# Second layer's attention: maxima's tiles padded with zeros to 128 partitions and columns, and the maxima rounded and split with two small reductions

## The reference, cut to what matters

```python
qk, v = jnp.split(x @ W_emb.T, 2, axis=-1)          # 16 heads of 64
anchor_B = qk @ W_anchor.T * SCALE                   # b, head, n, 64 anchors
attn = jax.nn.softmax(anchor_B, axis=-1)             # over the anchors
s = jnp.sum(attn, axis=-2)
out = jnp.einsum('bhna,bhnd->bhad', attn, v)         # gathered per anchor
out = recip[..., None] * out                         # recip = 1 / s
out = jnp.einsum('bhna,bhad->bhnd', attn, out)
return out.transpose(0, 2, 1, 3).reshape(b, n, INNER) @ W_out.T + b_out
```

## Time and profile before

| | |
|---|---|
| Median of 3 runs | 780.24 us (776.69 to 781.25) |
| Profiled execution, first to last instruction | 778.5 us |
| Mean granted TensorE clock, as a share of 2.4 GHz | 0.926 |
| TensorE matmuls busy | 654.1 us, 84% |
| VectorE busy | 570.3 us, 73% |
| ScalarE busy | 400.4 us, 51% |
| GpSimd busy | 277.6 us, 36% |
| Attention loops, from the span's start | about 303 to 363, 434 to 477, 548 to 591, 662 to 705 us |

### The profile page before, as it was taken

The page is one execution under the profiler, slowest core; times in us unless marked ns, Lnnn a source line. Parts: engine busy times, 40 slices in busy tenths (PEclk is TensorE's granted clock), DMA queues, the critical chain, the costliest instruction groups (busy, mean ns, idle before and its releaser), DMA issues.

```text
span 778.5 us, 9648 instructions
## 1 busy us (share of the span) xinstructions
PE 654.1 (84%) x2985; PEld 470.0 (60%) x2985; DVE 570.3 (73%) x1441; ACT 400.4 (51%) x698; POOL 277.6 (36%) x229
## 2 busy tenths in 40 slices
PE   5777550399999995879989899899899899899897
PEld 2666540388878883446468555478555478556575
DVE  4889959279866736996976786866796866783763
ACT  3646233277777732334375444485443585442573
POOL 6457778200000026686202375211485120341100
PEclk9979755699999985989999999999999999999999
DMA  6441587778898610001000000000100000000000
GB/s 212 136 177 52 202 296 275 233 250 267 250 304 307 215 58 27 18 21 28 0 1 0 35 28 21 1 0 1 41 23 20 0 1 1 27 1 1 0 1 28
DMA packets 25779, 69.26 MB, mean 89 GB/s; under 512 B 5296, under 2 KB 8384, under 8 KB 24384
## 3 DMA queue, kind: packets, MB, share of 16 engines
q1 hardware_dynamic: 21632, 60.24, 23.0%
q0 software_dynamic: 4096, 8.40, 3.6%
HBM read 46.46 MB, written 22.16 MB: 88 GB/s over the span
## 4 chain that ended last, share of the span: by engine, by line
PE 58%; DVE 21%; POOL 7%; issue 6%; DMA 4%; ACT 4%; SPq 1%; DVEq 0%; ACTq 0%; POOLq 0%
PE ps L1685 14%; PE ps L1687 8%; PE ps L1681 8%; PE ps L1942 6%; PE ps L1689 6%; PE ps L1688 6%; DVE stats L1061 3%; POOL rows_by_expert L605 3%; PE ps L1960 2%; PE ps L1930 2%; DMA wbuf<-w_split 2%; DVE ring L1565 2%; DMA raw<-in_w 1%; DVE yb L1465 1%; DVE cmat L1641 1%
## 5 line engine op out<-in xcount | busy, mean ns | idle before, releaser
L652 POOL DMA_INDIRECT yb<-y_by_expert,ypos x64 | 63.3, 989 | 158.2 <-DMA y_by_expert<-ysb 142.6
L1685 PE MATMUL ps<-hid,fh 128*128 128x512 f32 x256 | 103.5, 404 | 5.1 <-DVE hid L1549 5.1
L1687 PE MATMUL ps<-hid,fh 128*128 128x512 f32 x256 | 101.4, 396 | 0.0
L605 POOL DMA_INDIRECT rows_by_expert<-h,pos x64 | 71.1, 1112 | 25.0 <-issue 18.9
L700 POOL TENSOR_TENSOR misc<-misc,ring 128x1024 f32<-128x1024 f32 x28 | 66.0, 2357 | 33.8 <-DVE ring L1539 28.7
L1549 DVE TENSOR_TENSOR hid<-ring,hid 128x512 fp32r<-128x512 f32 x56 | 38.6, 689 | 41.7 <-ACT hid L941 40.1
L1942 PE MATMUL ps<-ring,hn 128*128 128x512 f32 x112 | 56.5, 628 | 5.3 <-DVE ring L1539 5.3
L1685 PEld LDWEIGHTS ps<-hid,fh 128*128 128x128 f32 x256 | 48.2, 188 | 21.0 <-DVE hid L1549 10.3
L1960 PE MATMUL ps<-attnT,cmat 128*128 128x512 f32 x128 | 56.9, 592 | 0.0
L1687 PEld LDWEIGHTS ps<-hid,fh 128*128 128x128 f32 x256 | 48.3, 188 | 10.7
L998 ACT ACTIVATE ring<-ps 128x1024 f32<-128x1024 f32 x32 | 32.8, 1025 | 42.6 <-PE ps L1930 42.4
(11 more groups left out here) (326 smaller groups left out, 1702.4 us busy)
## 6 DMA issues: line engine op xcount, KB each, us to landing
wbuf<-w_split SPq DMA_DIRECT2D x46, 512.0 KB, 5.6
w_split<-parts SPq DMA_DIRECT2D x4, 2048.0 KB, 7.7
raw<-in_w SPq DMA_DIRECT2D x8, 512.0 KB, 8.5
xs<-rows_by_expert SPq DMA_DIRECT2D x16, 256.0 KB, 5.4
y_by_expert<-ysb SPq DMA_DIRECT2D x16, 256.0 KB, 4.5
ffn_raw<-in_ffn SPq DMA_DIRECT2D x1, 2816.0 KB, 11.1
rows_by_expert<-zeros SPq DMA_DIRECT2D x9, 256.0 KB, 2.5
xa<-in_x SPq DMA_DIRECT2D x4, 512.0 KB, 4.9
```

The costliest lines, as they stand in the source:

```text
L605: gp.indirect_dma_start(disp, bass.IndirectOffsetOnAxis(pos[:, b, k, t:t + 1].bitcast(U32), 0), h1[:, b % 2, t, :], None).then_inc(scatter ...
L652: gp.indirect_dma_start(yb[:, k, t, :], None, ydisp, bass.IndirectOffsetOnAxis(ypos[:, b, k, t:t + 1].bitcast(U32), 0))\
L1685: te.matmul(out_, w(0), x(0), start=first, stop=False)
L1687: return te.matmul(out_, w(0), x(1), start=False, stop=last_)
```

## The change

Three things are changed together.

- `m32`, `mTs` and `onehot` become 128 wide or 128 high. `m32` is filled with zeros once (a memset of 128x256 on VectorE behind the cast of `onehot`), and `oh_f` is made on 128 partitions. So the transpose of the maxima loads 128 columns of weights in place of 32, the copy moves 128 partitions, and the two matmuls of `shift` use 128 rows of weights in place of 32.
- `neg_max` writes the negated maxima straight into `m32[:, i, 32:48]`. The cast becomes a reduction with a maximum over one element, negated, which writes the rounded maximum (positive now) as fp32r. The subtraction becomes a reduction with a sum over the pairs (rounded, negated maximum). The first 16 rows of `onehot` become -1 to match. The negated maxima in columns 32 to 47 meet rows of `onehot` that are zero. The wait for the transpose of tile t-2 moves from ahead of the cast to ahead of the first reduction.
- `upto` moves into the arena, to make room.

```diff
-        onehot = sb("onehot", [32, 1024], F32R)
+        onehot = sb("onehot", [128, 1024], F32R)
-        mTs = sb("mTs", [32, 128], F32R)
+        mTs = sb("mTs", [128, 128], F32R)
-        nmax = sb("nmax", [128, 2, H])
-        m32 = sb("m32", [128, 2, 2 * H], F32R)
+        m32 = sb("m32", [128, 2, 128], F32R)
-        oh_f = at("oh_f", 48, [32, 1024])
+        oh_f = at("oh_f", 48, [128, 1024])
+        upto = at("upto", 78, [128, 2 * E, 2 * E])
...
-                gp.affine_select(out=v, in_=v, compare_op=ALU.not_equal, fill=1.0, base=base,
+                gp.affine_select(out=v, in_=v, compare_op=ALU.not_equal, fill=1.0 if base else -1.0, base=base,
...
-                copy(mTs[:, :], ps[0:32, 1, 0:128]).then_inc(*act_maxT.raise_(t))
+                copy(mTs[:, :], ps[:, 1, 0:128]).then_inc(*act_maxT.raise_(t))
...
             v.tensor_copy(onehot[:, :], oh_f[:, :])
+            v.memset(f(m32[:, :, :]), 0.0)
...
                 if t >= 2:
                     dve.wait_ge(*dve_max.now(t - 2, b))
-                settle(b, v.tensor_reduce(nmax[:, i, :], ps[:, k0:k0 + 2, :].rearrange("p k (h a) -> p (k h) a", a=A),
-                                          X, ALU.max, negate=True))
-                if t >= 2:
                     dve.wait_ge(*pe_maxT.now(t - 2, b))
-                settle(b, v.tensor_copy(m32[:, i, 0:H], nmax[:, i, :]))
-                v.tensor_tensor(m32[:, i, H:2 * H], nmax[:, i, :], f(m32[:, i, 0:H]), ALU.subtract)\
-                    .then_inc(*dve_max.raise_(t))
+                rounded, minus = m32[:, i, 0:H], f(m32[:, i, 2 * H:3 * H])
+                settle(b, v.tensor_reduce(minus, ps[:, k0:k0 + 2, :].rearrange("p k (h a) -> p (k h) a", a=A), X, ALU.max,
+                                          negate=True))
+                settle(b, v.tensor_reduce(rounded, minus.unsqueeze(2), X, ALU.max, negate=True))
+                both_ = f(m32[:, i, 0:4 * H]).rearrange("p (k h) -> p h k", k=2)[:, 0:H, :]
+                v.tensor_reduce(f(m32[:, i, H:2 * H]), both_, X, ALU.add).then_inc(*dve_max.raise_(t))
...
-                transposes(1, [f(m32[:, t % 2, :])], 32).then_inc(*pe_maxT.raise_(t))
+                transposes(1, [f(m32[:, t % 2, :])]).then_inc(*pe_maxT.raise_(t))
```

More of the change, by code:

```diff
@@ L160, in build @@
         thr = sb("thr", [128, E])
-        upto = sb("upto", [128, 2 * E, 2 * E])
         unit = sb("unit", [128, NT])
@@ L1677, in _, with transposes @@
             te = nc.tensor
-            def transposes(bank, srcs, rows_=128):
+            def transposes(bank, srcs):
                 for i, s in enumerate(srcs):
-                    last_ = te.transpose(ps[0:rows_, bank, i * 128:(i + 1) * 128], s, ident[:, :])
+                    last_ = te.transpose(ps[:, bank, i * 128:(i + 1) * 128], s, ident[:, :])
                 return last_
```

## The result

The changed kernel takes 770.68 us in the median of four runs (770.13 to 770.90), the kernel before 778.47 in the four runs that stand against it (776.00 to 781.25). The ratio is 0.9905, interval 0.9878 to 0.9931: 7.8 us less in the medians, 5.4 to 9.5 by the interval, just short of the 1% that a measurement of this kernel tells from no change. The profiled execution spans 768.4 us at a clock of 0.926, against 778.5 before.

What follows compares the result with a forecast made beforehand. TensorE was taken to bound mid-loop, VectorE and GpSimd the loop ends and first batch. Gains of 1.5 + 1.5 + 2.3 + 0.8 less 0.3 made 5.8 us, from 780.24 to 774.4; range 770.5 to 779.5.

Steps and rivals of the forecast that it cites:

- the rival without a collision: Attention loops: the gather L652 does not wait for VectorE's L1539; batches 2 and 3 gain 2.3 each, 772.1 us; chance 0.22.
- half of 0.22 and a fifth of 0.50: Shares of the no-collision rival's and the forecast's chances taken as below 772.4 us, over 1% faster; stated total 0.24.
- Part 1, rows: TensorE's `shift` matmuls: 128-row weights remove the idle gaps of 0.36, 0.38 us per tile, step from 5.15 to 4.77.
- The rival by which the gaps stay: TensorE's shift: the 0.36 gaps are not caused by 32 rows and remain; only the casts count, 778.8 us; chance 0.18.
- 4 x 0.38 = 1.5 us a batch: Attention loops: the shorter TensorE step counts for `shift(2)` to `shift(5)`, the four ahead of the last logits.
- Part 2: VectorE's maxima: reductions of 0.17 and 0.19 us never wait for GpSimd; 0.1 gained at tile 6, 0.7 at the last.
- What is late next, batches 2 and 3: Loop ends: L652 waits for L1539, so L700 starts 0.85 late; of 2.3 us, 1.5 is gained in each batch.
- First batch: First attention loop: the 2.77 us cast goes but GpSimd bounds next; 0.8 us gained.
- that of tile 7 follows directly: First loop's end: tile 7's L700 starts right behind tile 6's, which ends at 359.7, and runs until 362.05.
- The lock-step: GpSimd and VectorE catch each other every round: L1539 ends 1.1 behind L700, L652 0.83 behind that, as in first batch.
- the rival by which it also sets in in batches 2 and 3: Later loops: rounds take 5.55 instead of 5.15, 2.5 us lost in each of batches 2 and 3; 783.2 us; chance 0.10.
- Setup: Ahead of the loops: VectorE's memset precedes the L1414s and delays scatter L605; its whole time, 0.3 us, is added.

Runs made afterwards that it cites:

- after_again: The changed kernel, unchanged, run again on a second chip; ratio to the kernel before 0.9932, loops 55.08, 41.07, 41.07, 40.26 us.
- after_cols32: The changed kernel with the maxima's transposition writing 32 columns again and the copy 32 rows, the shift keeping 128 rows; ratio to the kernel before 0.9962.
- pad_only: The kernel before with the zeros and 128 rows and columns, the cast and the subtraction kept; ratio to the kernel before 1.0009.
- subtraction_kept: The changed kernel with the pair-sum reduction replaced by a tensor_tensor addition of 16 elements, the rounding still a reduction; ratio to the kernel before 0.9957.
- one_each: The changed kernel with one gather instead of two in rounds 3, 4 and 5, three left behind the last L700; ratio to the kernel before 0.9879.
- memset_only: The kernel before with only the 128x256 memset added ahead of the L1414s and `m32` widened to hold it; ratio to the kernel before 1.0030.
- reductions_only: The kernel before with the two reductions in place of cast and subtraction, 32 rows and columns, no memset; ratio to the kernel before 0.9983.

## Why the prediction was right, and where it was not

The time, 770.68, lies inside the range, 0.2 above its lower end and 3.7 under the forecast, outside the 772.5 to 776.5 that the forecast gave itself; by the number alone the rival without a collision (772.1) was nearer, and only the traces speak against it. The prediction's base was the median of three runs then shown, 780.24; with the runs of this comparison it is 778.47, which is 1.8 of the 3.7. Against 778.47 the gain was 7.8, not 5.8; after_again on another chip has 0.9932 of 802, 5.5. From the start of the first loop to the end the two traces differ by 469.93 - 464.20 = 5.7. The 0.3 that the forecast took off for the memset lies ahead of the loops, so its 6.1 for the loops stands against this 5.7. They are that near in part by luck: the loops gave 5.2, for the first fell short by 1.3, and 0.5 came between and behind the loops, where no term stood. What the whole time gained beyond 5.7, 2.1 in the medians and 4.4 in the traces, came ahead of the loops, where the prediction had a loss; its cause stays open. (A slip in the chances: half of 0.22 and a fifth of 0.50 make 0.21, not 0.24.)

- *Part 1, rows.* Right: both gaps gone, the step 4.79, 2.7 us less of matmuls for 7 tiles, 0.38 each, and the columns free (after_cols32). The rival by which the gaps stay is refuted.
- *Part 1, what it is worth.* "4 x 0.38 = 1.5 us a batch" as a term of its own was wrong. Alone it is worth 0.1 (pad_only). The step read the earlier trace rows and thought that TensorE, alone on the path in mid-loop, was the only bound; VectorE and GpSimd had a ring of 5.35 beside its 5.15, not on the path only because they had started with slack. The chain of waits doesn't show a second bound that near; the casts growing by 0.2 a tile did, had I asked why they grow.
- *Part 2.* 170 and 186 ns against 0.17 and 0.19; the last tile's wait gone. But the wait was put down to the cast. The subtraction would have taken it over (subtraction_kept), so the second reduction, costed at nothing gained, is worth 0.7 in batches 2 and 3 and 1.4 in the fourth.
- *What is late next, batches 2 and 3.* Right. `scaled(6)` was to end 2.3 earlier and did by 2.4 (34.02 behind the loop's start, against 36.42), the second gather ends 0.83 behind L1539 (the first one caught takes 1.76, the later ones 0.98, where 1.03 to 1.1 were given), L700 starts behind it, 1.6 is left instead of 2.4. Batch 4, without gathers, keeps 2.4 (forecast 2.3). one_each, which takes the collision away, brings the two to 40.28 too. This refutes the rival without a collision, and with it the Trainium skill's inference (SBUF — State Buffer, Who interferes with whom) that a tensor_tensor leaves the writing of descriptors alone: here the second L651 waits 0.8 for the end of a tensor_tensor.
- *First batch.* Wrong: 0.8 less was forecast, 0.5 more came (0.47 and 0.51 in two pairs of traces). The failed step is "that of tile 7 follows directly". The L700s come at the times worked out there, 5.57 apart against 5.55; but the last L1539 is itself caught:

```profile
352.56 3.94 DVE L1539 TENSOR_TENSOR ring<-ring,lrec 128x1024 f32<-128x1024 f32 x1
```
```profile
352.08 0.95 POOL L651 DMA_INDIRECT yb<-y_by_expert,ypos  x1 [0.30 <-issue]
353.05 2.35 POOL L699 TENSOR_TENSOR misc<-misc,ring 128x1024 f32<-128x1024 f32 x1
356.57 2.35 POOL L699 TENSOR_TENSOR misc<-misc,ring 128x1024 f32<-128x1024 f32 x1 [1.17 <-DVE ring L1539]
```

  It was issued 0.49 ahead of L699, but under the gather that runs until 353.03, and ends 1.1 behind L699; so the L699 of tile 7 starts 1.17 later than "directly". Measured from the loop's start, the L699 of tile 6 ends at 51.20, where the prediction has 51.1, and that of tile 7 at 54.72 against 53.45: these 1.17 are all but 0.1 of the miss. The prediction used these very 1.1 for every earlier tile. The lock-step that it saw in this loop thus ran on for one tile more; the rival by which it also sets in in batches 2 and 3 (0.10) did not come.
- *Setup.* The memset takes 0.27 (0.3 was taken). The scatter's end, 138.58, was read as just behind the last L1414's, but it stands 0.84 behind the third's. That its time is added whole was wrong: in the traces of the same two chips with it the scatter of 5.83 us is gone, 2.5 less up to the last scatter. How much of that reaches the end stays open; memset_only, with a ratio of 1.0030 [0.9990, 1.0070] on the first chip, excludes a gain of over 0.1% there, but its scatters had ended early.
- *Between the loops* the kernel after is 0.1 shorter each time, 0.4 in all; no term stood for it, and no run looked for its cause. It shows in every kernel that has the pads and the cast replaced, as far as no late gather stretches the time there (but for one stretch of 71.5 in after_cols32), and in neither pad_only nor reductions_only.

## What to carry to other kernels

A cheap operation that waits for another engine can hold a whole ring of waits together: ask of every stretched instruction whether its length grows from tile to tile, for then a second bound is just beside the first and edits to either alone give little. Where two edits remove two bounds that near, try the pair before throwing either away; here 0.1 and 0.5 a loop alone made 1.6 to 2.4 together. And when a wait goes, look at what it kept apart: the gathers that stood well before had to be moved to keep the whole gain.

## What the runs showed of the hardware that I had not expected

- A tensor_tensor of 16 elements on VectorE (176 ns alone) takes up to 784 ns when GpSimd's tensor_tensor of 1024 elements runs, ending 0.03 behind it; a reduction of the same 16 elements takes 170 ns under the same instruction.
- A VectorE tensor_tensor of 1024 elements that starts under a running indirect DMA's issue, 0.49 ahead of the GpSimd tensor_tensor that follows it, waits for that too: 3.94 us instead of 1.23, ending 1.10 behind it (five kernels). No trace has the same start with GpSimd idle.
- An indirect DMA's issue can slip in at the first boundary of back-to-back tensor_tensors of VectorE (1.63 us) or be shut out through three of them (5.83) or four (7.49). It was shut out in all four traces without the memset ahead of them, and in none with it. The instant of issue alone doesn't explain it, and the cause is open.
- Weights of 32 rows among 128-row ones cost 0.38 us for one excursion of two matmuls; weights of 32 columns cost nothing that a loop's length shows (40.97 against 41.07).
- The kernel before took 777, 802 and 809 us on three chips. In its two traces, of 778.5 and 799.8, the first transposition of xs stands at 146.2 and 170.2 us, so all of the difference lies ahead of it; the loops agree to 0.02 us.
